# The low halves of the contexts ahead of the masking passes, and the odd graph's output ahead of the values

## What is computed

```python
h = jnp.maximum(_layernorm(x, axis=-1), 0.0)
q, k, v = _heads(h @ Wq + bq), _heads(h @ Wk + bk), _heads(h @ Wv + bv)
scores = jnp.einsum('bhqd,bhkd->bhqk', q, k) / np.sqrt(HEAD_SIZE)
bias = jnp.where(graph_mask, 0.0, NEG)[:, None]
probs = jax.nn.softmax(scores + bias, axis=-1)
ctx = jnp.einsum('bhqk,bhkd->bhqd', probs, v)
x = x + (heads_side_by_side(ctx) @ Wf + bf)
```

## Time and profile before

| | |
|---|---|
| median of 3 runs | 1950.31 us (1949.54 to 1950.85) |
| profiled execution | 1948.68 us |
| its span | 1946.9 us |
| TensorE busy | 1838.3 us |
| VectorE busy | 1640.3 us |
| ScalarE busy | 1549.7 us |
| GpSimd busy | 1485.0 us |

### The profile page before, as it was taken

One profiled execution on the slowest core, in us unless ns is written; L12 is line 12 of the kernel. 1 busy time (PEld: TensorE's weight loads), 2 busy tenths in 40 slices (PEclk: granted clock), 3 DMA queues, 4 the chain that ended last, 5 costly groups with the idle time before them and its releaser, 6 DMA issues.

```text
span 1946.9 us, 54319 instructions
## 1 busy us (share of the span) xinstructions
PE 1838.3 (94%) x17210; PEld 1040.0 (53%) x17210; DVE 1640.3 (84%) x5555; ACT 1549.7 (80%) x4789; POOL 1485.0 (76%) x1777
## 2 busy tenths in 40 slices
PE   8899999999999999999999999999999999999998
PEld 3455555555555555555555555555555555555554
DVE  7988888888888888888888888888888888888876
ACT  5768878888887888788788888888887888788874
POOL 4568887887788788878878887887888788778762
PEclk8999999999999999999999999999999999999999
DMA  6556666666666666666666666666666666665555
GB/s 198 166 151 186 196 190 185 183 193 192 195 184 190 187 189 196 196 185 181 194 191 195 190 186 181 189 197 194 183 190 186 193 191 191 182 185 174 177 166 187
DMA packets 439942, 363.32 MB, mean 187 GB/s; under 512 B 207700, under 2 KB 406888, under 8 KB 439656
## 3 DMA queue, kind: packets, MB, share of 16 engines
q1 hardware_dynamic: 439656, 359.86, 61.5%
HBM read 184.30 MB, written 175.37 MB: 185 GB/s over the span
## 4 chain that ended last, share of the span: by engine, by line
PE 56%; DVE 33%; issue 7%; POOL 1%; DMA 1%; SPq 1%; ACT 1%; DVEq 0%; POOLq 0%; ACTq 0%
PE ps_shared L665 13%; PE ps_shared L667 12%; PE ps_shared L666 12%; DVE probs L1289 11%; PE ps_qk L665 6%; PE ps_qk L667 6%; PE ps_qk L666 6%; DVE p_blocks L1230 6%; DVE ct_lo L1263 6%; DVE h_blocks L1230 3%; DVE stats L1225 3%; DVE qk_lo L1269 1%; DVE x_tile L1300 1%; SPq L367 1%; DMA p_dram<-p_blocks 1%
## 5 line engine op out<-in xcount | busy, mean ns | idle before, releaser
L540 POOL TENSOR_TENSOR probs<-probs,row_rcp 128x768 f32<-128x768 f32 x252 | 371.3, 1473 | 308.9 <-DVE row_rcp L1254 308.9
L986 ACT ACTIVATE probs<-probs,row_min 128x128 f32<-128x128 f32 x1512 | 582.8, 390 | 2.5 <-DVE row_min L1289 2.5
L1289 DVE CUSTOM_DVE_ANT_0 probs<-ps_scores,mask,minus_scale 128x128 f32<-128x128 f32 x1512 | 430.9, 348 | 1.7 <-issue 1.2
L552 POOL TENSOR_TENSOR p_half<-p_moved,p_half 128x768 f16<-128x768 f32 x236 | 387.4, 1642 | 2.0 <-ACT p_half L961 2.0
L1300 DVE SCALAR_TENSOR_TENSOR x_tile<-ps_shared,out_scale,x_tile 128x384 f32<-128x384 f32 x256 | 157.9, 617 | 229.6 <-PE ps_shared L667 224.5
L948 ACT ACTIVATE v<-ps_shared 128x384 f16<-128x384 f32 x236 | 115.6, 490 | 262.2 <-PE ps_shared L667 262.2
L665 PE MATMUL ps_shared<-wv_hi,ht_hi 128*128 128x384 f16 x756 | 246.8, 326 | 81.4 <-DVE ct_lo L1263 81.4
L1269 DVE SCALAR_TENSOR_TENSOR qk_lo<-ps_qk,qk_bias,qk_hi 128x512 f16<-128x512 f32 x384 | 276.0, 745 | 39.8 <-ACT qk_hi L969 39.5
L986 ACT ACTIVATION_READ_ACCUMULATOR probs<-probs,row_min 128x1 f32 x1512 | 287.0, 190 | 0.0
L969 ACT ACTIVATE qk_hi<-ps_qk,qk_bias 128x512 f16<-128x512 f32 x384 | 257.6, 671 | 14.7 <-PE ps_qk L667 14.6
L536 POOL TENSOR_TENSOR x_tile<-x_tile,out_bias 128x384 f32<-128x384 f32 x256 | 257.5, 1007 | 1.1 <-DVE out_bias L1213 1.1
(11 more groups left out here) (144 smaller groups left out, 3967.3 us busy)
## 6 DMA issues: line engine op xcount, KB each, us to landing
p_dram<-p_blocks SPq DMA_DIRECT2D x256, 384.0 KB, 2.4
p_moved<-p_dram SPq DMA_DIRECT2D x1024, 96.0 KB, 2.4
h_dram<-h_blocks SPq DMA_DIRECT2D x252, 192.0 KB, 2.5
h_moved<-h_dram SPq DMA_DIRECT2D x1008, 48.0 KB, 2.0
x_tile<-in_x SPq DMA_DIRECT2D x128, 192.0 KB, 2.8
out_x<-x_tile SPq DMA_DIRECT2D x128, 192.0 KB, 2.5
adj_u<-in_adj SPq DMA_DIRECT2D x64, 64.0 KB, 2.5
wv_raw<-in_L_gnn_Wv SPq DMA_DIRECT2D x2, 576.0 KB, 4.7
```

The lines of the kernel that those rows point to most:

```text
L540: nc.gpsimd.tensor_tensor(probs_of(t, i), probs_of(t, i), row_rcp[i % 2][:, :].rearrange("p (a o) -> p a o", o=1) .to_broadcast([P, HEADS, ...
L552: nc.gpsimd.tensor_tensor(p_part(i, 1), p_moved[i % 2][:, :, :].rearrange("p a n -> p (a n)"), p_part(i, 0), ALU.subtract).then_inc(p_set, 1)
L986: ins = nc.scalar.activation(tile[:, s, :], tile[:, s, :], ACT.Exp, bias=row_min[i % 2][:, s:s + 1], scale=-1.0, accum_out=row_sum[i % 2][ ...
L1289: ins = nc.vector.tensor_tensor_reduce(tile[:, s, :], score_bank(i, s // PAIRS)[:, (s % PAIRS) * P:(s % PAIRS + 1) * P], mask[b][:, i, :], ...
```

## The change

It reorders two queues. On VectorE, `ctx_lo` of the two graphs of the pair, which exists in even steps, comes ahead of `mask_and_min`. On TensorE, in even steps, `output` of the odd graph comes ahead of `project_v`; in odd steps nothing is moved. Nothing is added or removed, on these engines or elsewhere, and `last_units` is as it was.

```diff
@@ -806,9 +806,11 @@
                     if exists(t + 1):
                         for piece in PIECES[i][0] + PIECES[i][1]:
                             project_qk(t + 1, piece)
+                    if i % 2 == 0 and exists(ou):
+                        output(ou, oi)
                     if exists(t + 1):
                         project_v(t + 1, i)
-                    if exists(ou):
+                    if i % 2 and exists(ou):
                         output(ou, oi)
 
             def last_units():
@@ -1324,11 +1326,11 @@
                             statistics(su, si)
                     if exists(eu):
                         invert_sums(eu, ei)
-                    if exists(t):
-                        mask_and_min(t, i)
                     for cu, ci in pair_at(t, i):
                         if exists(cu):
                             ctx_lo(cu, ci)
+                    if exists(t):
+                        mask_and_min(t, i)
                     if t == 1:
                         weights_lo(1, CAST_ORDER[i])
                     if exists(t + 1):
```

## The result

The changed kernel took 1885.93 us (median of four runs, 1884.18 to 1886.24) against 1949.99 for the kernel before: a ratio of 0.967, interval 0.965 to 0.969, faster by 64 us. Forecast were 1892 us and a range of 1857 to 1914. The profiled execution took 1886.24.

A forecast was written before the change was run, and what follows sets the result against it. A loop of TensorE's output, VectorE's 5.3 us and TensorE was taken to set the period. TensorE's 28.04 us plus 0.62 wait makes 28.66 a slot against 29.66; 58 us saved over 58 slots gives 1892 us, range 1857 to 1914.

The forecast's parts named there:

- The stall of 0.79: TensorE's values product in even steps waits for VectorE's `ct_lo`, costing 0.79 us; `ctx_lo` ahead of the masks removes it.
- counting by starts: Losses on TensorE taken from instruction starts, 0.79 us per stall, not from idle rows, 0.63, which would give 1913 us.
- The masks' delay: VectorE's masks in even steps run up to 1.01 us later; hidden, since ScalarE reads them only in the next step.
- A new wait, once per slot: In step 3, the next slot's scores on TensorE wait 0.62 us for the last `qk_lo`, behind ScalarE's late `v_hi`.
- The chain through ScalarE: ScalarE's odd step: `v_hi` starts 0.26 us after the last values product; the last `qk_hi` ends 5.68 us after that start.
- The rest of the run: First slots and last units: taken as 0 change, with bounds of 5 us to gain and 2 to lose.
- the three hand-overs: Delays of 0.26, 0.03 and 0.16 us between engines before the late scores; leaving them out would give about 1866 us.
- The thin margins of step 1: TensorE's contexts, after the late odd step, find `v_lo` and the residual ready with 0.03 and 0.06 us to spare.
- the rival with waits in both pairs: Both margins in step 1 fail, each pair of steps loses some 0.6 us: 1928 us, half of it 1910; chance 0.18.
- The full gain: ScalarE's odd step runs 0.62 us faster, no score waits, 28.04 us a slot: 1856 us; chance 0.12.
- The slower one, by late transfers: Returned probabilities land 3.5 us later than reckoned, delaying ScalarE's `p_hi`, last chunk and scores: 1996 us; chance 0.05.
- VectorE's waits: In odd steps VectorE waits no longer for the output but for the exponentials at its inversion, 10.71 us after S.

The follow-up runs named there:

- lows_only: The changed kernel with TensorE's values again ahead of the output in even steps, so only VectorE's reorder is kept: 1854.73 us, ratio 0.951.
- output_step0: The changed kernel with output ahead of values in step 0 alone, values first again in step 2: 1856.87 us, ratio 0.952.
- output_only: The changed kernel with VectorE's `ctx_lo` back behind the masks, so only TensorE's reorder is kept: 1961.92 us, ratio 1.006.
- copy_step1: The changed kernel with one idle ScalarE copy of 256 columns, read by nothing, added in step 1: 1897.67 us, ratio 0.973.

## Why the prediction was right

**The stall of 0.79 goes.** Right. No wait for `ct_lo` is left in the steady part, and `lows_only` shows the full worth: a slot falls from 29.66 to 28.05, 94 us over 58 slots, as worked out, and 96 us on the medians of its chip. It also bears out counting by starts: the rows of idle time held 77.4 us, and removing them gave 94, 0.14 more for each of the 116 waits. The Trainium skill ("Trainium Kernel Development and Optimization", Performance Expectations) says that matmul busy time is a bad metric of the distance to roofline because matmuls are pipelined; of idle rows it says nothing there, but here they mislead by the same overlap.

**The masks' delay is hidden.** Right: `lows_only` has it, and its slot of 28.05 is TensorE's own work of 28.04.

**A new wait, once per slot.** Right in place, count and cause. The cause was shown three ways: without the output's move it is absent; with the move in step 0 alone it is too, but for 2 waits; and it follows ScalarE's queue ahead of the last chunk's copy, growing by about the 0.30 that is added there and all but going when the copy comes 1.0 earlier.

**Its size, 0.62.** The term that was mis-sized: it is 14.55 - 14.02 = 0.53. The chain through ScalarE was exact (0.26, then 5.68). What was off is the last hand-over, from the end of one engine's record to the start of the next one's: I took the 0.16 seen between `ct_lo` and the values product, and the score starts 0.06 after `qk_lo` ends. 58 slots at 0.09 are 5 us. That this is nearly all of the 6 between 1892 and 1886 is partly luck, for two smaller terms cancel. The rest of the run, which I took as unchanged, got 2 us longer, within my bound of 2 to lose. And I added 1.6 us from the profiled execution to the median, while here the median lies 0.3 below it.

The Trainium skill ("Perfetto Trace Analysis", Per-instruction lifecycle) says that semaphore waits and propagation lie outside the profiled window, and gives no length for them. Leaving the three hand-overs out would have given 1866; they belong in, each from its own pair of engines and lines.

**The thin margins of step 1.** The margin for `v` held, and not by luck alone: it was 0.11 where I had 0.03, since this hand-over too is 0.06 and not 0.16. Still, the rival with waits in both pairs was only 0.1 us of ScalarE's work away.

**Rivals.** The full gain did not come with this change, but is had without its second part. The slower one, by late transfers, did not occur: in the steady part ScalarE never waits for `p_moved`. It does wait for `h_moved`, which before it did 4 times:

```profile
ACT v L950 <- PE ps_shared L667: 246.4, 113, 2.8
ACT ht_hi L942 <- DMA h_moved<-h_dram: 13.5, 26, 1.0
```

These are 26 waits with 13.5 us, and nothing of it reaches TensorE: the scores' wait is 0.5 at the longest and 26.7 / 58 = 0.46 on average, and no product waits for anything else. The path of this rival is real all the same. In `output_step0` the longest wait of the scores, 1.2 us, comes behind a step in which ScalarE stood idle twice for late transfers:

```profile
609.64 0.84 ACT L963 ACTIVATE p_half<-p_moved 128x768 f16<-128x768 f32 x1 [0.57 <-DMA p_moved<-p_dram]
...
612.21 0.52 ACT L942 ACTIVATE ht_hi<-h_moved 128x384 f16<-128x384 f32 x1 [0.55 <-DMA h_moved<-h_dram]
```

VectorE's waits are as forecast, for the exponentials at the inversion and for the last chunk, and, which I had not listed, for the high half of the values (`v_hi`, whose tile the rows call `v`):

```profile
DVE row_rcp L1256 <- ACT probs L988: 68.3, 112, 2.7
DVE qk_lo L1271 <- ACT qk_hi L971: 61.6, 140, 1.4
DVE v L1260 <- ACT v L950: 58.2, 95, 1.0
```

The inversion came 10.85 after S (990.07) and not 10.71, without effect: the `qk_lo` behind the masks started at 12.60, and the last one still had 0.39 to wait.

**What stays open.** Whether the 96 us of `lows_only` can be exceeded by another order was not tried: TensorE waits for nothing there in the steady part, and only its own work is left.

## What to carry to other kernels

Two reorders made together should be priced apart: here the first removed the whole stall, and the second only moved a producer later. Moving an operation back by 1.5 us is free only if the whole queue behind its consumer has that room; ask which instruction of the consumer's step is needed first elsewhere, and put it first. An idle copy of known length is a cheap probe of slack: 0.30 us cost 18 us in one place, 12 in another and nothing in a third.

## What I had not expected of the hardware

The hand-over from VectorE to TensorE is not one number: 0.16 us from the end of `ct_lo` to the values product in the kernel before, 0.06 from the end of `qk_lo` to the scores after. The producer does not set it. In `output_only` the same `ct_lo` hands over to the output: the pair takes 1.02 and one of them 0.55, so the first, started at 1005.98, ends at 1006.53, and the output starts at 1006.59, again 0.06 later. What differs is on TensorE. The values product waits for two semaphores, and in the trace of the kernel before its wait for `ct_set` (L704) is an instruction of its own, 51 ns long, between the end of `ct_lo` (1016.03) and the load of the weights (1016.16):

```profile
L704 PEldq EVENT_SEMAPHORE  x1: 51/51/51, 1016.1 to 1016.1; - x1
```

At the three hand-overs of 0.06 (`qk_lo` to the scores, `ct_lo` to the output, `v` to the contexts) the weight load takes the wait itself: the list of waits puts its idle time down to VectorE there (49.0 us in 58 waits for `qk_lo` in the changed kernel), and down to "issue" at the 116 values products of the kernel before. No run has the values product without that instruction, so that it accounts for the whole 0.1 is argued and not shown.

And a short wait can be missing from the list of a product's waits. In `copy_step1` the contexts' wait for `v` stands on the weight load (16.1 us in 56 waits) and has no row on the products. Their own idle time is some 0.1 us a slot, while no list here shows a wait under 0.2: so the list of the products' waits leaves out what costs 12 us of the run.
